# Splitting and spreading the read-out matmuls of a state-space scan, and loading the next chunk's rows ahead of the picks

## The reference

```python
delta = softplus(delta @ dt_proj_w.T + dt_proj_b)
A = -jnp.exp(A_log)
def step(h, inp):
    dt, b, xt, c = inp
    dA = jnp.exp(dt[:, :, None] * A)
    h = dA * h + dt[:, :, None] * b[:, None, :] * xt[:, :, None]
    y = jnp.einsum('bdn,bn->bd', h, c)
    return (h, y)
_, ys = jax.lax.scan(step, h0, xs)
```

## Time and profile before

| | us |
|---|---|
| three runs | 1347.94, 1350.41, 1356.02 (median 1350.41) |
| the profiled execution | 1350.97 |
| its span | 1349.1 |
| the scan stage in it, chunks 1 to 31 | 118.7 to 723.1 |

### The profile page before, as it was taken

The page is one execution under the profiler, slowest core; times in us unless marked ns, Lnnn a source line. Parts: engine busy times, 40 slices in busy tenths (PEclk is TensorE's granted clock), DMA queues, the critical chain, the costliest instruction groups (busy, mean ns, idle before and its releaser), DMA issues.

```text
span 1349.1 us, 29055 instructions
## 1 busy us (share of the span) xinstructions
PE 1126.4 (83%) x11730; PEld 726.6 (54%) x11730; DVE 846.0 (63%) x1006; ACT 500.5 (37%) x1245; POOL 306.3 (23%) x930
## 2 busy tenths in 40 slices
PE   3647787889878887788886499999999597999998
PEld 2535444444444554454543288887777344465665
DVE  5859989899999999899995211112111477842211
ACT  3865554556555655555553011111111110121110
POOL 9641222222223222422232211111111200000000
PEclk8865868776888779876877599999999797999999
DMA  3897235433223222312214652222210400000000
GB/s 105 244 281 209 61 87 134 107 98 103 52 58 90 47 51 56 90 36 48 59 50 155 203 200 79 77 93 94 97 43 16 133 1 0 0 8 8 17 16 16
DMA packets 171685, 111.99 MB, mean 83 GB/s; under 512 B 93637, under 2 KB 162248, under 8 KB 169248
## 3 DMA queue, kind: packets, MB, share of 16 engines
q1 hardware_dynamic: 163120, 88.69, 23.7%
q0 software_dynamic: 8000, 20.87, 4.7%
q10 hardware_dynamic: 432, 0.59, 0.2%
HBM read 63.18 MB, written 45.90 MB: 81 GB/s over the span
## 4 chain that ended last, share of the span: by engine, by line
PE 52%; DVE 21%; issue 9%; SPq 7%; ACT 5%; DMA 3%; POOL 2%; DVEq 0%; POOLq 0%; ACTq 0%
DVE h L1151 13%; PE psum L1401 10%; PE psum L1413 10%; PE psum L1885 8%; PE psum L935 5%; PE psum L1896 4%; PE psum L921 4%; ACT decay L1036 3%; PE psum L902 3%; DVE den L1715 2%; PE psum L1841 2%; SPq L278 2%; DMA xdiag<-x_parts_d 1%; SPq L201 1%; SPq L199 1%
## 5 line engine op out<-in xcount | busy, mean ns | idle before, releaser
L1151 DVE TENSOR_TENSOR_SCAN h<-decay,psum 128x1024 f32<-128x1024 f32 x256 | 568.6, 2269 | 41.9 <-ACT psum L1046 34.5
L1036 ACT ACTIVATE decay<-psum 128x512 f32<-128x512 f32 x512 | 279.2, 600 | 211.1 <-PE psum L902 108.8
L921 PE MATMUL psum<-xdiag,bstat 96*128 96x64 bf16 x4096 | 199.9, 211 | 59.3 <-DVE h L1151 57.9
L921 PEld LDWEIGHTS psum<-xdiag,bstat 96*128 96x128 bf16 x4096 | 166.0, 109 | 86.7 <-DVE h L1151 77.3
L902 PEld LDWEIGHTS psum<-rows,shared 32*128 32x128 bf16 x4096 | 90.0, 104 | 221.2 <-issue 114.2
L935 PE MATMUL psum<-h,cstat 128*32 128x512 f32 x1024 | 187.2, 814 | 1.0 <-ACT y_raw L1088 1.0
L902 PE MATMUL psum<-rows,shared 32*128 32x64 bf16 x4096 | 123.9, 207 | 46.5 <-ACT decay L1036 38.0
L1401 PE MATMUL psum<-xdt,shared 128*128 128x320 f32 x512 | 141.4, 438 | 0.7 <-ACT xdt L1460 0.7
L1306 POOL TENSOR_TENSOR carry<-decay,h 128x16 f32<-128x16 f32 x240 | 57.9, 241 | 366.6 <-ACT decay L1036 366.4
L1413 PE MATMUL psum<-shared,hid 128*128 128x256 f32 x640 | 139.5, 379 | 0.6 <-ACT hid L1454 0.6
L1413 PEld LDWEIGHTS psum<-shared,hid 128*128 128x128 f32 x640 | 121.2, 190 | 17.0 <-issue 1.1
(11 more groups left out here) (192 smaller groups left out, 1044.1 us busy)
## 6 DMA issues: line engine op xcount, KB each, us to landing
shared<-in_w SPq DMA_DIRECT2D x16, 1024.0 KB, 4.8
xdiag<-x_parts_d SPq DMA_DIRECT2D x256, 48.0 KB
x_parts_d<-x_parts POOLq DMA_DIRECT2D x46, 256.0 KB, 8.0
parts_d<-dt_parts SPq DMA_DIRECT2D x24, 256.0 KB, 9.4
rows<-parts_d SPq DMA_DIRECT2D x128, 48.0 KB
disp_d<-zero SPq DMA_DIRECT2D x4, 1305.0 KB, 8.2
xd<-disp_d SPq DMA_DIRECT2D x8, 652.5 KB, 6.2
picked_d<-zero SPq DMA_DIRECT2D x4, 1024.0 KB, 5.7
```

Of the source, the lines that this page charges most:

```text
L921: ins = pe.q.matmul(to.rearrange("p d (s e) -> p s d e", e=2), bstat[0:ROWS, c % 2, b, :], xdiag[0:ROWS, c % 2, b, :, d, :], start=True, s ...
L1036: act.q.activation(decay[:, gi % NB, 8 * half:8 * half + 8, :], per_d(bank_a[half]), ACT.Exp).then_inc(sem("exp"), 1)
L1151: dve.q.tensor_tensor_scan(out=h[:, half_slot(c, half), ch:ch + G, :].rearrange("p d t -> p (d t)"), data0=decay[:, gi % NB, :, :].rearran ...
```

## The change

The read-out is cut into eight half lumps: each has the same 4 matmuls with 256 moving columns, one half of the state. They are issued in all seven groups after the chunk, two of them in the fourth. The next chunk's rows load in three pieces, in groups 0 to 2, and the picks move from position 8 to 9 in the order, behind the loads. The last chunk's read-out, after the scan, takes the half lumps two by two.

```diff
-LOADS = ((("dt", 0), ("dt", 1), ("dt", 2)), (("dt", 3), ("b", 0), ("b", 1)), (("x", 0), ("x", 1)), (("x", 2), ("x", 3)),
-         (("x", 4), ("x", 5)), (("x", 6), ("x", 7)))
+LOADS = ((("dt", 0), ("dt", 1), ("dt", 2), ("dt", 3), ("b", 0), ("b", 1)), (("x", 0), ("x", 1), ("x", 2), ("x", 3)),
+         (("x", 4), ("x", 5), ("x", 6), ("x", 7)))
...
-Y_STEPS = ((0,), (), (1,), (), (2,), (), (3,))
-Y_OUT, Y_PICK = 7, 8
+Y_STEPS = ((0,), (1,), (2,), (3, 4), (5,), (6,), (7,))
+Y_OUT, Y_PICK = 7, 9
...
-    for js in (js for js in Y_STEPS if js):
+    for js in ((0, 1), (2, 3), (4, 5), (6, 7)):
...
-                first, last = sorted((half_slot(c, 0), half_slot(c, 1)))
-                for j in js:
+                slots_of_h = sorted((half_slot(c, 0), half_slot(c, 1)))
+                for half, j in (divmod(n, 4) for n in js):
                     for q in range(4):
                         tok = 16 * q + 4 * j
-                        ins = pe.q.matmul(bank_y[32 * q:32 * q + 32, :].rearrange("p (s d e) -> p s d e", s=2, e=4),
-                                          s["cstat"][:, tok // 4, :], h[:, first:last + 1:last - first, :, tok:tok + 4],
+                        to = bank_y[32 * q:32 * q + 32, 256 * half:256 * half + 256].rearrange("p (d e) -> p d e", e=4)
+                        ins = pe.q.matmul(to, s["cstat"][:, tok // 4, :], h[:, slots_of_h[half], :, tok:tok + 4],
                                           start=j == 0, stop=j == 3)
-                if js[-1] == 3:
+                if js[-1] == 7:
                     ins.then_inc(sem("y"), 1)
```

## The result

In 15 runs of each, side by side, the kernel before took 1355.32 us and the changed kernel 1363.51 us: the ratio is 1.0064, with a 95% interval of 1.0046 to 1.0083, that is 8.7 us slower (6.2 to 11.2). The profiled execution of the changed kernel took 1360.80 us; its span is 1359.3 us.

The account below looks back on a forecast made before the run. VectorE sets the scan stage's pace; its 36.6 us idle was put down to TensorE's quantity of work at the lower clock level. Terms -4 + 4 - 3 + 8 = +5 us on 1350.97 gave 1356 us, range 1336 to 1377.

Parts of the forecast that it names:

- The loads, -4 us: Scan stage, chunks 2, 5 and 7: loads issued ahead of picks end waits for xdiag, gaining 4 us.
- The cut, +4 us: Read-out in halves: extra instruction starts and three more groups with TensorE changes per chunk cost 4 us at the lower level.
- Evenness, -3 us: Scan stage: halves avoid scans made late by a whole lump in one group, gaining 3 us (0 to 8).
- The clock, +8 us: Scan stage: fewer whole lumps to raise TensorE's clock; lower level's share goes from 44% to some 53%, costing 8 us.
- part 1: The forecast's term for loads ahead of picks: waits for xdiag in chunks 2, 5 and 7 go, gaining 4 us.
- The clock holds: Rival: read-out in seven of eight groups keeps TensorE's clock up, lower level's share 25%, 1329 us; chance 0.12.
- The clock stays down: Rival: without whole lumps the lower level lasts for 75% of the scan stage, 1381 us; chance 0.18.
- The picks come late: Rival: delayed picks make TensorE wait at L970 in 15 odd chunks, +15 us, 1371 us; chance 0.07.
- The clock as before: Rival: clock unchanged; loads win 4 us, halves cost 4, evenness wins 3, 1348 us; chance 0.25.

Follow-up runs that it names:

- in pairs: Kernel before with its lumps cut into halves issued two by two in the old groups, old loads and picks: 0.9990, 1349.89 us.
- the even kernel: Changed kernel with one half lump in each of eight groups, none with two, copy-out one group later: 1.0351 of the kernel before, 1402.32 us.
- halves in pairs: Changed kernel, new loads kept, with half lumps issued two by two in the whole lumps' old groups 2, 4, 6 and 0: 0.9916, 1339.37 us.
- double in group 4: Changed kernel with its two-half group moved from group 5 to group 4: 0.9965 of the kernel before, 1345.04 us.
- one half left out: Changed kernel without half lump 3, an eighth of the read-out, partial sums not added up: 1.0118 of the kernel before, 1371.32 us.
- pairs with filler: Half lumps two by two in the old groups, new loads, plus four unread matmuls in groups 1, 3, 5, 7 from chunk 3: 0.9842, 1330.11 us.
- double in group 2: Changed kernel with its two-half group moved from group 5 to group 2, behind the empty group 1: 1.0013, 1356.91 us.

## Why the prediction was right, and where it was not

The time, 1363.5 us against 1356 with a range of 1336 to 1377, came out inside one per cent of no change, on the slower side. About 4 of the 7.5 us between 1356 and 1363.5 are the base: the kernel before took 1355.32 us beside the change, not 1350.97. Against it the sum said +5 and +8.7 was measured. Of the four terms two were too high, together by some 10 us, and one was too low by about as much, so that the total came out near is in good part luck; the clock's term was about right.

**The loads, -4 us.** The step was right and its size too small: the loads alone gave -8.5 us (5.5 to 11.5). The prediction took half of the 7.8 us of waits, "since in chunk 7 VectorE felt 1.6 us less than TensorE waited". It had looked at one scan. In chunk 7 the next scan is late as well, by 1.25 us, and in chunks 2 and 5 it is 1.3 and 1.9 us in two scans each: 7.1 us of idle time, which the loads alone take away. The mechanism in the earlier trace rows, the big DMA ahead of two small ones, was the main part of it, as moving that DMA alone shows (6.6 us). The waits in chunks 2, 5 and 7 are gone, as said.

**The cut, +4 us.** Too high; in pairs it is -1.4 us (-3.6 to +0.9). A single half at the lower level took 205.52 - 204.51 = 1.01 us to L902's start, within the 0.94 to 1.05 foretold; at the upper one 304.34 - 303.73 = 0.61 in the even kernel, over the 0.56. Against half a whole lump that is 0.07 us more at the lower level and 0.11 at the upper, and only where halves stand alone. The Trainium skill, "TensorEngine Tiling (Array Packing)", Key Properties, would drain TensorE at each change of tiling mode; the spread halves have three more groups a chunk with such changes, and these 0.07 to 0.11 us leave little room for a price. The row in which the prediction looked for one, L902's weight loads waiting for nothing named, went from 106.7 to 41.0 us with more changes instead of fewer. By that rule the sum was 8 us higher; this term would have been further off.

**Evenness, -3 us.** This is the step that failed, in sign. The prediction said that "the quantity explains the whole idle time, so little is left for placement", and set down the double half's place in group 5 in one sentence without a price. The change has 22.6 us of its idle time right behind that group, and moving the double half one group forward gives 13.4 us back at nearly the same clock, 0.76 against 0.74. The sign named for this part failed too: single scans are 1.37 us late behind one half in chunks 11, 19 and 27, where it stands beside routing matmuls. Spreading costs 14.7 to 20 us; less what 10 to 12 points more at the lower level cost at 8.7 us a tenth, the places account for +4 to +11 us (an estimate), where -3 stood. The price was to be had from the rows: 3.59 us for a double and 0.4 us or more for the transposes against 2.27 us for a scan, in each odd chunk that is at the lower level there.

**The clock, +8 us.** The share went from 44% to 52%, where 53% was forecast, and the mechanism is what the runs confirm: without a double or whole lump the lower level lasts for 74 to 80% of the stage. The price of 8.7 us for each tenth is right in size and not a constant, as far as single profiles of kernels that also differ in their places can tell. From halves in pairs (42%, 27.2 us idle) to double in group 4 (48%, 31.7 us) it is 7.5 us a tenth; from the pairs to one half left out (74%, 54.5 us) 8.5; but from pairs with filler (16%, 19.8 us) to pairs without it only 2.8. PEclk came out at 0.74 where 0.73 was forecast, and the waits for L1046 at 37.5 us where it said 38. But the idle time of 36.6 us is not all TensorE's quantity: 7.1 us of it were the loads', which the prediction had also counted as part 1, so that its 38 us met the 36.6 was to that extent luck. (The 5.7 us of waits for GpSimd in the earlier trace rows are not part of it: 5.5 of them stand ahead of the first scan of all, at 100.85 us, before the stage begins.)

**The sum.** Loads -8.5, cut -1.4, and spreading +14.7 (1.0099 / 0.9990, with the old loads) to +20 us (1.0064 / 0.9916, with the new): +5 to +10 us, against +8.7 measured. The forecast's evenness and clock together made +5 where 15 to 20 were measured; the loads and the cut made 0 where -10 was. The total came out 4 us too low because the errors cancel nearly.

**The rivals.** "The clock holds" is refuted for this change; the share at the lower level rose. The Trainium skill, "TensorE: Matmul & The Clock Gate", Why this matters for your kernels, advises against idle gaps between bursts; the rows agree in the kernel with fillers, where the gaps were filled and the clock went to 0.92. The change has no long gaps to avoid: in the 4 us before its level fell at 196.7 us, TensorE's gaps were 0.50 to 0.59 us. Cutting the read-out finer does not fill gaps: at the upper level every group gets one of some 0.6 us instead of every second group a longer one. "The clock stays down" did not come true here, but its mechanism did in the even kernel, at 80% and +47 us: with the double half taken away the change goes there too (74% with one half left out). "The picks come late" is refuted: L970 has no wait for y_sb in the scan stage (the 3.0 us one behind it, for the last chunk, was 3.2 us before). In chunk 15 the picks are issued at 391.76 us for 2.42 us and the transposes come at 401.15, 7.0 us later, more than the 6.3 us of before: SP issued the eight loads at 388.22, ahead of the picks, and the picks were not late for it. "The clock as before" had the loads too small and the placement wrong.

**What stays open.** In the profile of the changed kernel the scan at the start of chunk 16 is 3.67 us late and the third one 2.37 us, while several engines show short pieces of work with waits that the profile does not explain:

```profile
411.55 2.29 DVE L1151 TENSOR_TENSOR_SCAN h<-decay,psum 128x1024 f32<-128x1024 f32 x1 [3.67 <-issue]
```

A stall of the kind is there at the same chunk in the kernel with one half left out (2.64 and 2.85 us), in the even one (2.64 and 2.14), with the double in group 2 (1.54, 1.47 and 1.32) and, once, with the zeroing DMA moved (2.02); not in the profiles of before, of the loads or the read-out alone, of the pairs, of the double in group 4 or of the fillers. GpSimd issues indirect DMAs at this time, but it does so in the kernel before as well. No run tells its cause. It is 6 us of the profiled execution, and may be part of the difference between +4.8 and +8.7 us.

## What to carry to other kernels

Where an engine's clock follows its load, cost a reordering in three parts: how much of the stage runs at each level, which piece of work brings the level back, and which groups then stand at the end of the slow stretch; here the piece that ends it cost most where it shared its group with other work. Smoothing the load of an engine that has slack at its upper level can lower the clock and so make the load too much for it; adding matmuls in the gaps did the opposite and won 0.7%. And on an in-order DMA queue look first for one big transfer ahead of small ones that somebody waits for: moving that one alone was worth 0.5%.

## What was unexpected in the hardware

- Less work was slower: leaving out an eighth of the read-out moved the lower level's share from 52% to 74% and the ratio from 1.0064 to 1.0118.
- More work was faster: 464 matmuls added (928 records on the page, 13682 against 12754) moved that share from 42% to 16% and the ratio from 0.9916 to 0.9842.
- TensorE busy for 94% of the stage (621.5 of 657.9 us) went with the lowest clock, 0.60, and busy for 85% (496.5 of 585.0 us) with the highest, 0.92: in these kernels the busy share says nothing of the level, since the lower level makes the same work last longer.
- Two records of 256 fp32 columns take as long as one of 512, once the instructions stand back to back: 1.94 us for 16 and 1.94 us for 8 at the lower level.
